# Non-local attention block: turned diagonal tiles split into two halves, and four chunks of g made at once in the head

## The chip, the cores and the metric

One core of one Trainium2 chip. The metric is the time of one execution in microseconds (us), median of several. TensorE multiplies matrices, VectorE and ScalarE work element by element, GpSimd too, and SyncE issues the DMAs.

## The reference

For each of 4 images x of 256 channels and n = 64 x 64 = 4096 places, after a group norm over 32 groups:

```python
g_x  = einsum('oc,bchw->bohw', g_w, x) + g_b          # 128 channels
f    = einsum('bnc,bcm->bnm', theta, phi)             # theta = x transposed, phi = x: f is symmetric
attn = softmax(f, axis=-1)
y    = einsum('bnm,bmc->bnc', attn, g_x)
wy   = einsum('oc,bchw->bohw', W_w, y) + W_b
wy   = batch_norm(wy) * gamma + beta                  # over images and places
out  = x + (wy + group_norm(x))
```

All arrays are fp32. The work lies in f (4096 x 4096 per image) and in attn times g.

## The kernel before

**Blocks and tiles.** The 4096 places are cut into NB = 8 chunks of W = 512. Block j computes y for the 512 places of chunk j. It takes TPB = 32 steps, one for each tile of 128 x 512 of the softmax's numerator; a step is numbered p = 32 j + i. Since f is symmetric, only the chunks (j, c) with c >= j are multiplied (`multiply`, L1135 to L1137). A product goes in three parts, high x high, high x low and low x high, each in the type fp32r; the halves of x are xh and xl. VectorE takes each product out of PSUM into a ring of 9 slots in SBUF (`take_f`, L930) and keeps a running maximum (L938); chunks with c > j are also spilled to DRAM.

**Two kinds of tiles.** `tile(p)` gives block, chunk, row and whether the tile is "left".
- A right tile is exponentiated on ScalarE in the ring (L760), turned by four transposes on TensorE into a PSUM bank (`turn`, L1177) and then split: ScalarE casts it to its high half phi (`split_hi`, L786), VectorE subtracts that from the bank to get the low half plo (`split_lo`, L965), and TensorE makes three products, gh x phi, gl x phi, gh x plo (L1205 to L1207). gh and gl are the halves of g.
- A left tile is already the way round that is needed. It is loaded from the spill (into lbuf or the free parts fy_c and fy_d), GpSimd subtracts the row maxima (L695), ScalarE exponentiates (`exp_left`, L775), and TensorE takes it in one fp32 product with the unsplit g, gf (L1201), which leaves two records in the trace. VectorE adds the left tiles up for the softmax's denominator (`add_left`, L978 for the first two, L982 for the others).
- The diagonal chunk (j, j) is symmetric in itself, so in blocks 1 to 6 its four tiles need no turning either. `turned_self` marks them: they are left tiles that stay in the ring. They are the turned diagonal tiles of the title, used in the first third of a block.

**What sets the order.** Every engine runs its own list of steps written out by the planners at the file's head; the engines meet only in semaphores. In step p TensorE turns the tile of step p + LAG (LAG = 2), makes the products planned for this step, and then calls `attend` for tile p. ScalarE at step s exponentiates left tile s + 3 and casts tile s + 2. VectorE at step p makes the low half of tile p first, then adds left tiles for step p + 1, takes products, and near a block's begin makes the reciprocal of the last block's sums (`invert`, L995, L998, L1000), which TensorE spreads in L1263. phi has 3 buffers, plo 2, products 2 banks. In the second half of the first three images the next image's statistics (L873), high and low halves (L736, L668) and first products come in between.

**The head.** Before the first step there are the statistics and halves of image 0 and the 32 products of its block 0. g is made in half chunks (`make_g`, L1157 to L1160) into the one bank sps, which VectorE empties into gf (`add_g`, L911) before the next one is made. `NEXT_G` is the chunks 0 and 1, made before the steps; chunks 2 to 7 are made at the steps that G_AT names, chunks 2 and 3 at steps 2, 3, 6 and 7, two steps' work ahead of their use. ScalarE casts a chunk to gh (`make_gh`, L750), GpSimd makes gl (L674).

## Time and profile before

| | |
|---|---|
| median of 3 runs | 2197.24 us (2196.96 to 2199.29) |
| profiled execution | 2195.28 us, span from first to last instruction 2193.5 us |
| granted TensorE clock, mean | 0.991 of full speed |
| TensorE busy | 2059.5 us, 94% |
| VectorE busy | 1556.7 us, 71% |
| ScalarE busy | 1090.8 us, 50% |
| GpSimd busy | 810.7 us, 37% |

The span is what the trace covers; the profiled execution's own time is 1.8 us longer. The engines work side by side, so their times don't add up. Matmul records overlap, since a record lasts until its result is out, while the next one has begun: what a matmul costs is read from start to start.

### The profile page before, as it was taken

The page shows a single profiled execution, that of the slowest core. Times are in us where ns is not written, and L with a number is a line of the kernel's source. Part 1 is how long each engine was busy: PE and PEld are TensorE (multiplying, and loading weights), DVE is VectorE, ACT ScalarE, POOL GpSimd, SP SyncE. Part 2 cuts the span into 40 slices and gives each one's busy share as a digit, 9 for nine tenths or more (in the row PEclk, how much of TensorE's full clock was granted, in tenths as well). Part 3 has the DMA queues.
Part 4 walks back from the last instruction along what each step waited for, and adds up shares of the span by engine and source line. Part 5 has one row for each costly group of instructions (what it writes and reads, how often), then busy time and mean ns, then how long its engine had stood idle before and what let it go on. Part 6 is the DMA issues. An engine that isn't in the chain of part 4 may idle for free.

```text
span 2193.5 us, 32307 instructions
## 1 busy us (share of the span) xinstructions
PE 2059.5 (94%) x9348; PEld 1454.6 (66%) x9348; DVE 1556.7 (71%) x3123; ACT 1090.8 (50%) x2234; POOL 810.7 (37%) x623
## 2 busy tenths in 40 slices
PE   5899999989999999999999999998999999999988
PEld 4686777755577777765667677765558777766433
DVE  5576777777766777786767677777776677777656
ACT  3344455555444445447444445545544444555644
POOL 3001223459602023448631122445850102345840
PEclk9999999999999999999999999999999999999999
DMA  3112234545512323554522223464541233346969
GB/s 139 77 77 81 103 121 130 173 150 178 178 45 87 115 98 110 165 175 138 197 72 93 87 92 112 129 200 137 191 150 49 87 120 102 110 130 218 344 236 356
DMA packets 108408, 304.50 MB, mean 139 GB/s; under 512 B 11584, under 2 KB 11968, under 8 KB 93888
## 3 DMA queue, kind: packets, MB, share of 16 engines
q1 hardware_dynamic: 108224, 302.30, 40.6%
q8 instruction: 84, 1.38, 0.2%
q14 instruction: 100, 0.82, 0.1%
HBM read 159.65 MB, written 142.61 MB: 138 GB/s over the span
## 4 chain that ended last, share of the span: by engine, by line
PE 68%; issue 11%; POOL 8%; ACT 5%; DVE 4%; DMA 3%; DVEq 0%; SPq 0%; POOLq 0%; ACTq 0%
PE bank L1201 12%; PE bank L1135 10%; PE bank L1137 9%; PE bank L1136 9%; PE bank L1177 7%; PE bank L1205 4%; PE bank L1207 4%; PE bank L1206 4%; POOL fy_d L695 3%; POOL fy_c L695 3%; ACT ring L760 2%; PE bank L1350 2%; PE bank L1271 2%; DVE plo L965 2%; DMA fy_c<-spill 2%
## 5 line engine op out<-in xcount | busy, mean ns | idle before, releaser
L786 ACT CAST phi<-bank 128x512 fp32r<-128x512 f32 x480 | 281.9, 588 | 765.7 <-PE bank L1177 764.7
L930 DVE TENSOR_SCALAR_CACHE_REDUCE ring<-bank 128x512 f32<-128x512 f32 x576 | 395.7, 688 | 209.3 <-PE bank L1137 164.0
L1135 PE MATMUL bank<-xh 128*128 128x512 f32 (+3 forms) x1152 | 512.8, 445 | 8.4 <-POOL xl L668 6.4
L1137 PE MATMUL bank<-xh,xl 128*128 128x512 f32 (+3 forms) x1152 | 436.1, 379 | 0.0
L965 DVE TENSOR_TENSOR plo<-bank,phi 128x512 fp32r<-128x512 f32 x480 | 327.2, 685 | 153.5 <-ACT phi L786 121.2
L1136 PE MATMUL bank<-xl,xh 128*128 128x512 f32 (+3 forms) x1152 | 433.1, 376 | 0.0
L1177 PEld LDWEIGHTS bank<-ident,ring 128*128 128x128 f32 x1920 | 231.6, 142 | 183.4 <-issue 109.2
L760 ACT ACTIVATE ring<-ring,nmax 128x512 f32<-128x512 f32 x480 | 345.8, 722 | 0.0
L1177 PE MATMUL bank<-ident,ring 128*128 128x128 f32 x1920 | 295.1, 277 | 43.7 <-DVE plo L965 22.5
L695 POOL TENSOR_TENSOR fy_d<-fy_d,maxrow 128x512 f32<-128x512 f32 x188 | 242.3, 1291 | 222.3 <-DMA fy_d<-spill 222.3
L695 POOL TENSOR_TENSOR fy_c<-fy_c,maxrow 128x512 f32<-128x512 f32 x200 | 259.0, 1297 | 167.0 <-DMA fy_c<-spill 166.6
L1135 PEld LDWEIGHTS bank<-xh 128*128 128x128 f32 x1152 | 218.1, 189 | 76.9 <-issue 29.3
L938 DVE TENSOR_TENSOR colmax<-bank,colmax 128x512 f32<-128x512 f32 x392 | 269.0, 686 | 0.0
L695 POOL TENSOR_TENSOR ring<-ring,maxrow 128x512 f32<-128x512 f32 x96 | 125.5, 1318 | 356.7 <-ACT maxrow L769 356.7
L1136 PEld LDWEIGHTS bank<-xl,xh 128*128 128x128 f32 x1152 | 219.0, 190 | 55.0 <-issue 29.2
L1137 PEld LDWEIGHTS bank<-xh,xl 128*128 128x128 f32 x1152 | 217.0, 188 | 42.1
L1205 PE MATMUL bank<-phi,gh 128*128 128x512 f32 x480 | 214.0, 446 | 19.2 <-DVE plo L965 18.8
L1201 PE MATMUL bank<-fy_c,gf 128*128 128x512 f32 x400 | 206.5, 599 | 4.2 <-DVE bank L982 3.0
L1201 PE MATMUL bank<-fy_d,gf 128*128 128x512 f32 x376 | 194.4, 599 | 4.7 <-DVE bank L982 3.7
L1207 PE MATMUL bank<-plo,gh 128*128 128x512 f32 x480 | 189.4, 394 | 0.0
L1206 PE MATMUL bank<-phi,gl 128*128 128x512 f32 x480 | 188.2, 392 | 0.0
L674 POOL TENSOR_TENSOR gl<-gf,gh 128x512 fp32r<-128x512 f32 x32 | 41.0, 1282 | 364.7 <-ACT gh L750 364.7
(115 smaller groups left out, 2716.9 us busy)
## 6 DMA issues: line engine op xcount, KB each, us to landing
spill<-ring SPq DMA_DIRECT2D x112, 1024.0 KB, 4.4
fy_c<-spill SPq DMA_DIRECT2D x200, 256.0 KB, 4.1
fy_d<-spill SPq DMA_DIRECT2D x188, 256.0 KB, 4.1
ring<-x_dram SPq DMA_DIRECT2D x40, 512.0 KB, 4.9
lbuf<-spill SPq DMA_DIRECT2D x60, 256.0 KB, 4.0
yd<-yn SPq DMA_DIRECT2D x32, 256.0 KB, 3.4
fx_a<-x_dram SPq DMA_DIRECT2D x16, 512.0 KB, 8.3
out_dram<-fx_a SPq DMA_DIRECT2D x16, 512.0 KB, 4.6
```

What stands on the lines that cost most here:

```text
L695: nc.gpsimd.tensor_tensor(left_at(w), left_at(w), maxrow[:, :], ALU.subtract).then_inc(left_sub, 1)
L760: nc.scalar.activation(ring[:, SLOT[u], t, :], ring[:, SLOT[u], t, :], ACT.Exp, bias=nmax[:, j % 3, t:t + 1], accum_out=rsum[:, j % 2, t, ...
L786: nc.scalar.copy(phi[:, HI_BUF[n], :], whole(p)).then_inc(hi_made, 1)
L930: last = nc.vector.tensor_scalar(ring[:, SLOT[u], t, :], src, 1.0, None, ALU.mult, ALU.max, accum_out=rowm[:, t, c:c + 1])
L965: nc.vector.tensor_tensor(plo[:, n % LOS, :], whole(p), phi[:, HI_BUF[n], :].bitcast(F32), ALU.subtract).then_inc(lo_made, 1)
L1135: nc.tensor.matmul(dst, xh[:, k, rows], xh[:, k, cols], start=(k == 0), stop=False)
L1136: nc.tensor.matmul(dst, xh[:, k, rows], xl[:, k, cols], start=False, stop=False)
L1137: last = nc.tensor.matmul(dst, xl[:, k, rows], xh[:, k, cols], start=False, stop=(k == K - 1))
L1177: last = nc.tensor.transpose(pps[:, n % 2, t * P:(t + 1) * P], ring[:, k, t, r * P:(r + 1) * P], ident[:, :])
L1201: nc.tensor.matmul(y, gf[:, c, r, :], left_at(LEFT_NO[p]), start=begin, stop=end).then_inc(tile_used, 1)
L1205: nc.tensor.matmul(y, gh[:, c, r, :], hi, start=begin, stop=False)
L1207: nc.tensor.matmul(y, gh[:, c, r, :], lo, start=False, stop=end).then_inc(tile_used, 1)
```

## The change

The turned diagonal tiles move from the list of tiles that are taken whole to SPLIT, the list of tiles that are cast, subtracted and taken in three products. They stay left tiles otherwise: GpSimd's subtraction, the exponential and the addition remain, and they are not turned by TensorE. Their source for the cast and the subtraction is the ring in SBUF (`whole`). SPLIT grows from 120 to 144 tiles per image. In the head the chunks 0 to 3 of g (FIRST_G) are made before the steps, the two half chunks of each in two banks, sps and lacc, and the casts to gh of chunks 0 and 1 stand behind six exponentials on ScalarE. lo_made counts in twos, with all its waits doubled.

```diff
-FULL = range(1, NB)
-SPLIT = [p for p in range(TILES) if not (tile(p)[3] and p // TPB in FULL)]
+SPLIT = [p for p in range(TILES) if not tile(p)[3] or turned_self(*tile(p)[:2])]
...
+FIRST_G = range(LAST_HEAD_G[0])
...
-            for c in NEXT_G:
-                make_gh(0, c, first=True)
             for s in range(FIRST_EXP, 0):
                 for x3 in EXPS_AT[s]:
                     exp_right(0, *x3)
+                if s + LAG == 0:
+                    for c in NEXT_G:
+                        make_gh(0, c, first=True)
...
+                made = lacc if first and h == 1 and c in FIRST_G else sps
+                nc.vector.tensor_reduce(gf[:, c, 2 * h:2 * h + 2, :], made.rearrange("p (t o c) -> p t c o", t=T // 2, o=2),
...
-                                        ALU.subtract).then_inc(lo_made, 1)
+                                        ALU.subtract).then_inc(lo_made, 2)
...
-                if p - 1 in G_AT:
+                if p - 1 in G_AT and not (first and G_AT[p - 1][0] in FIRST_G):
...
-            for c in NEXT_G:
+            for c in FIRST_G:
                 for h in range(2):
-                    add_g(0, c, h)
+                    add_g(0, c, h, first=True)
...
-                elif c + h > 0:
-
-                    pe.wait_ge(g_added, 2 * c + h)
+                elif c > 0:
+
+                    pe.wait_ge(g_added, 2 * c + h - (1 if c in FIRST_G else 0))
...
-                    pe.wait_ge(lo_made, b * NSPLIT + SPLIT_NO[p] + 1)
+                    pe.wait_ge(lo_made, b * (2 * NSPLIT) + 2 * SPLIT_NO[p] + 2)
...
-                if p in G_AT:
+                if p in G_AT and not (first and G_AT[p][0] in FIRST_G):
```

Where the instructions move: VectorE at the begin of block 5 (steps 161 to 163 of the loop over images), before. REGISTER_ALU rows compute the value of a wait; the line numbers of the changed file are 1 to 3 higher.

```order
L970 REGISTER_ALU
L978 TENSOR_TENSOR bank<-lbuf,ring 128x512
L992 REGISTER_ALU
L995 TENSOR_REDUCE lside<-bank 128x4
L998 TENSOR_TENSOR lsum<-lside,lsum 128x4
L1000 RECIPROCAL linv<-lsum 128x4
L928 REGISTER_ALU
L930 TENSOR_SCALAR ring,rowm<-bank 128x512
L938 TENSOR_TENSOR colmax<-bank,colmax 128x512
```

The same place on VectorE after the change:

```order
L967 TENSOR_TENSOR plo<-ring,phi 128x512
L972 REGISTER_ALU
L980 TENSOR_TENSOR bank<-lbuf,ring 128x512
L994 REGISTER_ALU
L997 TENSOR_REDUCE lside<-bank 128x4
L1000 TENSOR_TENSOR lsum<-lside,lsum 128x4
L1002 RECIPROCAL linv<-lsum 128x4
L930 REGISTER_ALU
L932 TENSOR_SCALAR ring,rowm<-bank 128x512
L940 TENSOR_TENSOR colmax<-bank,colmax 128x512
```

A subtraction with the inputs ring and phi now stands ahead of the first addition and of the reciprocal. Two more follow in steps 163 and 165, one in step 168.

ScalarE in the head, before (x6 is six instructions in a row):

```order
L736 CAST xh<-ring 128x2x512
L750 CAST gh<-gf 128x512 x2
L760 ACTIVATE ring,rsum<-ring,nmax 128x512 x6
L786 CAST phi<-bank 128x512
L760 ACTIVATE ring,rsum<-ring,nmax 128x512
```

And after:

```order
L736 CAST xh<-ring 128x2x512
L760 ACTIVATE ring,rsum<-ring,nmax 128x512 x6
L750 CAST gh<-gf 128x512 x2
L786 CAST phi<-bank 128x512
L760 ACTIVATE ring,rsum<-ring,nmax 128x512
```

The two casts of g moved behind the six exponentials.

## Rows read from the trace of the kernel before

**Rows 1.** The page: busy time, and the chain that ended last by engine

```profile
PE 2059.5 (94%) x9348; PEld 1454.6 (66%) x9348; DVE 1556.7 (71%) x3123; ACT 1090.8 (50%) x2234; POOL 810.7 (37%) x623
...
PE 68%; issue 11%; POOL 8%; ACT 5%; DVE 4%; DMA 3%; DVEq 0%; SPq 0%; POOLq 0%; ACTq 0%
```

**Rows 2.** Busy time by stretch: length, engines (instructions), clock, DMA share, GB/s

```profile
core 0: us, PE busy (x) PEld busy (x) DVE busy (x) ACT busy (x) POOL busy (x), PEclk, DMA share, GB/s
774.00:800.00 26.00, 25.83 (x128) 19.89 (x127) 19.68 (x42) 10.18 (x23) 7.47 (x6) 1.00 0.21 72
840.00:856.00 16.00, 16.00 (x80) 11.16 (x79) 11.85 (x24) 9.49 (x21) 9.96 (x9) 1.00 0.26 85
897.00:914.00 17.00, 17.00 (x83) 12.07 (x81) 13.40 (x26) 8.28 (x17) 12.30 (x11) 1.00 0.26 85
951.00:972.00 21.00, 18.00 (x75) 11.66 (x75) 19.70 (x40) 6.68 (x13) 14.36 (x13) 1.00 0.48 140
1013.00:1030.00 17.00, 14.86 (x55) 9.40 (x56) 13.77 (x25) 10.86 (x18) 17.00 (x13) 1.00 0.38 120
1984.00:1998.00 14.00, 13.96 (x69) 10.02 (x68) 10.58 (x24) 6.59 (x13) 13.96 (x11) 1.00 0.55 169
2031.00:2044.00 13.00, 11.54 (x43) 6.20 (x42) 8.93 (x15) 8.87 (x18) 10.82 (x9) 1.00 0.79 221
```

**Rows 3.** Groups by line and form: busy us, mean ns, idle before

```profile
L695 POOL TENSOR_TENSOR fy_c<-fy_c,maxrow 128x512 f32<-128x512 f32 x200 | 259.0, 1297 | 167.0 <-DMA fy_c<-spill 166.6
...
L1201 PE MATMUL bank<-ring,gf 128*128 128x512 f32 x192 | 98.2, 596 | 4.5 <-DVE bank L982 4.1
...
L978 DVE TENSOR_TENSOR bank<-lbuf,ring 128x512 f32<-128x512 f32 x20 | 27.8, 1390 | 0.4 <-ACT lbuf L775 0.3
...
L978 DVE TENSOR_TENSOR bank<-fy_c,lbuf 128x512 f32<-128x512 f32 x4 | 2.8, 704 | 0.0
L978 DVE TENSOR_TENSOR bank<-ring 128x512 f32<-128x512 f32 x4 | 2.8, 696 | 0.0
```

**Rows 4.** Timeline of TensorE: start, us from start to end

```profile
299.63 0.40 PE L1205 MATMUL bank<-phi,gh 128*128 128x512 f32 x1
...
300.32 0.60 PE L1177 MATMUL bank<-ident,ring 128*128 128x128 f32 x4
...
331.31 1.02 PE L1201 MATMUL bank<-lbuf,gf 128*128 128x512 f32 x2
332.17 1.02 PE L1201 MATMUL bank<-ring,gf 128*128 128x512 f32 x2
```

**Rows 5.** Timeline of all engines, block 5 of the second image

```profile
956.72 1.26 DVE L978 TENSOR_TENSOR bank<-lbuf,ring 128x512 f32<-128x512 f32 x1
...
957.39 1.71 POOL L695 TENSOR_TENSOR fy_d<-fy_d,maxrow 128x512 f32<-128x512 f32 x1
...
959.38 0.65 PE L1263 MATMUL bank<-ident,linv 128*128 128x128 f32 x4 [1.37 <-DVE linv L1000]
...
966.60 1.12 PE L1201 MATMUL bank<-ring,gf 128*128 128x512 f32 x2 [1.28 <-DVE bank L982]
```

**Rows 6.** Timeline of all engines, the head

```profile
76.67 0.39 PE L1157 MATMUL bank<-wgs,xh 128*128 128x256 f32 x1 [1.49 <-DVE gf L911]
...
82.56 0.62 ACT L750 CAST gh<-gf 128x512 fp32r<-128x512 f32 x1 [3.32 <-DVE gf L911]
...
86.06 1.97 PE L1177 MATMUL bank<-ident,ring 128*128 128x128 f32 x8 [4.26 <-ACT ring L760]
...
87.33 0.56 ACT L786 CAST phi<-bank 128x512 fp32r<-128x512 f32 x1
...
89.50 0.78 PE L1205 MATMUL bank<-phi,gh 128*128 128x512 f32 x1
...
97.86 0.28 PE L1157 MATMUL bank<-wgs,xh 128*128 128x256 f32 x1
...
98.79 0.60 PE L1177 MATMUL bank<-ident,ring 128*128 128x128 f32 x4
```

**Rows 7.** Busy time and granted clock (the number after POOL)

```profile
87.00:100.00 13.00, 12.28 (x65) 10.54 (x63) 5.18 (x10) 6.54 (x17) 0.00 (x0) 0.75 0.00 1
```

More of the change, by code:

```diff
@@ L906, in group, with add_g @@
                                             1.0, None, ALU.add).then_inc(gnp_made, 1)
-            def add_g(n, c, h):
+            def add_g(n, c, h, first=False):
                 dve.wait_ge(g_made, n * (2 * NB) + 2 * c + h + 1)
-                nc.vector.tensor_reduce(gf[:, c, 2 * h:2 * h + 2, :], sps.rearrange("p (t o c) -> p t c o", t=T // 2, o=2),
+                made = lacc if first and h == 1 and c in FIRST_G else sps
+                nc.vector.tensor_reduce(gf[:, c, 2 * h:2 * h + 2, :], made.rearrange("p (t o c) -> p t c o", t=T // 2, o=2),
                                         AX.X, ALU.add).then_inc(g_added, 1)
@@ L1149, in make_g @@
                     shared_free(b, "g", c, h)
-                elif c + h > 0:
-                    pe.wait_ge(g_added, 2 * c + h)
+                elif c > 0:
+                    pe.wait_ge(g_added, 2 * c + h - (1 if c in FIRST_G else 0))
+                made = lacc if first and h == 1 and c in FIRST_G else sps
                 for r in range(2 * h, 2 * h + 2):
                     rows = slice(c * W + r * P, c * W + (r + 1) * P)
-                    both = sps[:, r % 2 * 2 * CI:(r % 2 + 1) * 2 * CI]
-                    high = sps[:, r % 2 * 2 * CI:r % 2 * 2 * CI + CI]
+                    both = made[:, r % 2 * 2 * CI:(r % 2 + 1) * 2 * CI]
+                    high = made[:, r % 2 * 2 * CI:r % 2 * 2 * CI + CI]
                     nc.tensor.matmul(both, xh[:, 0, rows], wgs[:, 0, :], start=True, stop=False)
@@ L1171, in turn @@
                 if n >= 2:
-                    pe.wait_ge(lo_made, b * NSPLIT + SPLIT_NO[IN_PSUM[n - 2]] + 1)
+                    pe.wait_ge(lo_made, b * (2 * NSPLIT) + 2 * SPLIT_NO[IN_PSUM[n - 2]] + 2)
                 elif not first:
-                    pe.wait_ge(lo_made, b * NSPLIT + SPLIT_NO[IN_PSUM[n - 2]] + 1 - NSPLIT)
+                    pe.wait_ge(lo_made, b * (2 * NSPLIT) + 2 * SPLIT_NO[IN_PSUM[n - 2]] + 2 - 2 * NSPLIT)
                 k = SLOT[CHUNK_NO[j, c]]
@@ L1313, in _ @@
             pe.wait_ge(wg_lo, 1)
-            for c in NEXT_G:
+            for c in FIRST_G:
                 for h in range(2):
```

## The prediction

> **What bounds the kernel now.** I read the page first. TensorE is busy 94% of the span, VectorE 71%, and 68% of the chain that ended last is on TensorE [rows 1]. So work taken from TensorE should pay. But the chain also holds 8% GpSimd, 5% ScalarE and 4% VectorE: there are places where TensorE follows another engine. An average over the span hides the places of the change, so I went on to the view of busy time by stretches and asked for those in which the turned diagonal tiles are used, in blocks 2 to 6 of the second image and 5 and 6 of the last [rows 2]. There the picture differs by block: in block 2 VectorE has 19.68 of 26.00 us, in block 4 13.40 of 17.00, in block 5 19.70 of 21.00. In block 5 VectorE, not TensorE, is the full engine (TensorE 18.00 of 21.00). The reader is to see that the same edit meets a full TensorE in blocks 2 to 4 and a full VectorE or GpSimd in blocks 5 and 6.
>
> **The tiles on TensorE.** 96 tiles change (4 in each of 6 blocks and 4 images; the fp32 product leaves two records each, hence x192 in [rows 3]). In the timeline an fp32 product takes 0.86 us from its start to the next one's (331.31 to 332.17), and the three products of a split tile 0.69 us (299.63 to 300.32) [rows 4]. So TensorE gets 0.17 us per tile back, 16.3 us in all if it were the bound at each; that is the most the tiles can give. The mean of a record (596 ns) would have said 1.19 us for the fp32 product, since records overlap; starts are what counts.
>
> **The tiles on ScalarE and VectorE.** Each tile gets a cast to the high half on ScalarE, which stands at 50% in the page and is ahead in these stretches; I cost it at nothing. Its cover is the two steps by which the split runs ahead of the product; were that gone, the cast would cost its own length. Each tile also gets a subtraction on VectorE, 128x512, both inputs in SBUF. No such subtraction runs before, but an addition of this size and kind does, L978 [rows 3]: 696 ns with ring and ring, 704 with fy_c and lbuf, 1390 on average with lbuf and ring. The difference is GpSimd: the one at 956.72 took 1.26 us while GpSimd was inside a subtraction, and GpSimd's next one, at 957.39, took 1.71 us [rows 5] where 1.30 is the mean [rows 3]. The two engines exclude each other here. The mean over the 28 L978 instructions is (20 x 1.390 + 4 x 0.696 + 4 x 0.704) / 28 = 1.19 us. Bounds: 0.70 us when GpSimd is idle, 1.39 us where it is not. I take 1.19 us, since the new instructions stand in the very same stretches; 4 of them are 4.8 us per stretch (2.8 to 5.6).
>
> The Trainium skill, "SBUF — State Buffer on-chip working memory", section "Who interferes with whom", says the same and speaks against this change: a VectorE instruction with two SBUF inputs and a GpSimd one that reads SBUF lock each other out for a whole instruction. It says besides that an instruction with one SBUF input doesn't take part, so the existing split tiles, whose source is in PSUM, are no measure for the new ones: by their 0.69 us a stretch would get 2.8 us, by the rule up to 5.6. The trace agrees with the lock.
>
> Now stretch by stretch: VectorE's sum with 4.8 us more, against the stretch's length [rows 2]. Where it still fits, the stretch gets 4 x 0.17 = 0.7 us shorter; where it doesn't, it gets longer by the excess.
> - Block 2: 19.68 + 4.8 = 24.5 of 26.0. It fits with little room, so I count -0.3. Block 1 has no row here; it starts like block 2, with the fewest left tiles of all, and I let it fit: -0.7.
> - Block 3: 11.85 + 4.8 = 16.7 of 16.0: 0.7 too much, against 0.7 saved: 0.
> - Block 4: 13.40 + 4.8 = 18.2 of 17.0: +1.2; I take +1.
> - Block 5 (images 0 to 2): 19.70 + 4.8 = 24.5 of 21.0: +3.5. Here I also followed the order. The first new subtraction stands right ahead of L978 and the reciprocal chain [rows 5]. Both need the port, so after the first has waited for GpSimd, L978 waits for GpSimd's next instruction as well: the reciprocal (L1000) comes some 1.8 us later, and with it L1263 at 959.38, for which TensorE already sat idle 1.37 us. Two more subtractions stand before the addition that releases L1201 at 966.60, for which TensorE already waits 1.28 us. Together 1.8 + 2 x 1.1 = 4.0. I take +4.0.
> - Block 6 (images 0 to 2): 13.77 + 4.8 = 18.6 of 17.0, GpSimd busy 17.00 of 17.00: +1.8.
> - Block 5 of the last image, without the next image's statistics: 10.58 + 4.8 = 15.4 of 14.0: +1.5. Block 6: 8.93 + 4.8 = 13.7 of 13.0: +1.
>
> An image 0 to 2 thus gets -0.7 - 0.3 + 0 + 1 + 4.0 + 1.8 = +5.8 us, the last +2.5, together +19.9 us. What queues behind the subtraction on VectorE is the addition of the next left tile, the taking of the products out of PSUM and, at a block's begin, the reciprocal; TensorE waits for each.
>
> **The head.** Before, TensorE makes 4 half chunks of g, each waiting for VectorE to empty the only bank (the second starts at 76.67). ScalarE casts chunk 1 at 82.56, and only behind it come six exponentials, of which the first turning needs four; it starts at 86.06, the first cast of a tile at 87.33, the first product with a tile at 89.50 [rows 6]. From the end of the cast of chunk 1 (83.1) to 87.33 the six take 4.2 us. After the change they come first, from about 76.2 (VectorE releases the second half chunk at 76.67, right behind the row maxima), and end near 80.5. TensorE makes 8 half chunks in two banks. A half chunk is 0.93 us of TensorE (97.86 to 98.79) [rows 6]. The third starts at 76.67, where the second does now; from there one is made under VectorE's addition, so that two take some 1.95 us instead of one: the eighth ends near 82.5. From the first turning to the first product it takes 3.44 us now (86.06 to 89.50), at a low clock and with exponentials in between; I estimate 2.5 us at the full clock, so the first product comes at about 85.0, 4.5 us earlier. Four half chunks are gone from steps 2, 3, 6 and 7, where TensorE is full: 4 x 0.93 = 3.7 us. And the clock: from 87 to 100 us it is 0.75 on average [rows 7], so it is at 1.2 GHz for half of these 13 us, up to about 93.5; TensorE had sat idle 4.26 us before 86.06. The work from 89.5 to 93.5 would take 2.0 us, half, less at 2.4 GHz. Since TensorE now pauses for about 1 us only, I expect that it stays at 2.4 GHz. Head: -4.5 - 3.7 - 2.0 = -10.2 us (-8.2 if the clock falls again; -3.7 if ScalarE's new order brings nothing).
>
> The Trainium skill, "TensorE: Matmul & The Clock Gate", section "What's actually happening", puts the low clock down to idleness before it; by that rule the 2.0 us come back with the shorter pause, and the row agrees, with the low clock standing behind the 4.26 us.
>
> **The sum.** 19.9 - 10.2 = +9.7 us on the profiled execution's 2195.28 us (its span is 2193.5): 2205.0 us. The same sums with a subtraction at its lower bound (2.8 us per stretch) fit everywhere but in block 5: about -2 us an image and -4 in the last, tiles -10.2, in all 2175; at its upper bound (5.6) the tiles come to about +35, in all 2220. The median of the runs shown is 1.96 us above that execution, so I expect a median of 2207 us, 0.45% slower. A measurement of this kernel can tell about 0.2% (4.4 us) from no change.
>
> **The rivals.** (a) Faster: VectorE's extra work is absorbed. VectorE is idle 29% of the span and TensorE, not it, ends most waits; it may catch up in the steps behind each stretch. Then the tiles give between 0 and -16.3 us and the head -10.2: 2169 to 2185, most likely 2181 with the tiles at -4. For it: VectorE is idle 6.3 us of 26.0 even in block 2's stretch [rows 2]. Against: in block 5 TensorE already waits for VectorE [rows 5]. It decides if the tiles cost less than 5.7 us in all, that is if the stretches of blocks 5 and 6 grow by less than 1 us each instead of the 5.8 above for both.
> (b) The halves cancel: at 1.0 us for a subtraction (4.0 us per stretch) the tiles come to +2.8 us an image and +1 in the last, +9.4, against the head's -10.2: 2196, no change.
> (c) The lock hits in full: every subtraction waits for a whole GpSimd instruction and GpSimd, which is full in block 6, falls behind as well. At +4 us in blocks 4 and 6 and +6 in block 5: 4 x 13 = 52, less 6 in blocks 1 to 3, less the head's 10: 2197 + 36 = 2233.
> (d) The clock falls again inside the kernel: TensorE's new waits in block 5 (1.37 + 1.8 = 3.2 us before L1263) come near the 4.26 us after which the clock fell in the head. If it falls there, the work of the next 6.5 us or so runs at half speed, 3 us more in each of 3 images: 2216. The page "TensorE: Matmul & The Clock Gate" of the Trainium skill says that an idle stretch throttles.
>
> **How the numbers follow.** My forecast (+4.4 to +22 us) 0.50, (d) 0.07, (c) 0.08, (b) within 0.2% 0.14, (a) 0.21. Slower 0.65, same 0.14, faster 0.21. The range leaves out the deeper half of (a) and the upper half of (c): 2184 to 2226.
>
> **What would show it.** In the profile after: the three products at 0.69 us from start to start; the new subtraction on average at 1.0 to 1.3 us, longest in block 6, and GpSimd's at 1.7 where they meet; TensorE's first product with tiles near 85 us, with the clock near full from 75 to 100; the stretch of block 5 some 25 us instead of 21, the blocks 1 to 3 unchanged within 1 us each. Wrong would be: subtractions at 0.7 us throughout, a block 5 of the old length, or a head that comes no earlier because ScalarE stands in the casts of g in its new place.

## The result, and the profile after

| | before | after |
|---|---|---|
| median | 2197.39 us (4 runs, 2196.96 to 2199.29) | 2239.54 us (4 runs, 2236.23 to 2241.52) |
| ratio | | 1.0189, 95% interval 1.0171 to 1.0206 |
| span of the profiled execution | 2193.5 us | 2238.4 us |
| mean granted clock | 0.991 | 0.986 |

The change makes the kernel 1.9% slower. The direction was forecast; 2239.54 us lies above the range (2184 to 2226).

The page of the changed kernel, busy time by engine and the chain that ended last, against [rows 1]:

```profile
PE 2061.5 (92%) x9444; PEld 1480.9 (66%) x9444; DVE 1646.0 (74%) x3219; ACT 1143.9 (51%) x2330; POOL 826.5 (37%) x623
...
PE 64%; issue 13%; POOL 7%; DVE 7%; ACT 5%; DMA 3%; DVEq 0%; SPq 0%; ACTq 0%; POOLq 0%
```

VectorE has 89.3 us more work and is busy 74% instead of 71%: nothing here looks full. Of the 44.9 us that the span grows, TensorE's idle time (span less busy) takes 42.9: 134.0 us before, 176.9 after. VectorE's share of the last chain goes from 4% to 7% and TensorE's falls from 68% to 64%. The groups by line and form (busy us, mean ns, idle before with its releasers), against [rows 3]:

```profile
L967 DVE TENSOR_TENSOR plo<-bank,phi 128x512 fp32r<-128x512 f32 x480 | 327.0, 685 | 152.8 <-ACT phi L786 76.4 <-PE bank L1210 39.9 <-PE bank L1204 22.0
...
L695 POOL TENSOR_TENSOR fy_c<-fy_c,maxrow 128x512 f32<-128x512 f32 x200 | 267.0, 1337 | 166.3 <-DMA fy_c<-spill 166.0
...
L967 DVE TENSOR_TENSOR plo<-ring,phi 128x512 fp32r<-128x512 f32 x96 | 96.9, 1009 | 6.4 <-ACT phi L786 6.2
...
L980 DVE TENSOR_TENSOR bank<-lbuf,ring 128x512 f32<-128x512 f32 x20 | 29.7, 1484 | 0.0
```

The new subtraction (plo from ring) takes 1009 ns on average, the old one from PSUM 685. GpSimd's subtraction goes from 1297 to 1337 ns, the addition L980 from 1390 to 1484. The view of waits shows who waits for the low halves (us in all, number, longest):

```profile
PEld bank L1208 <- DVE plo L967: 105.0, 106, 2.8
...
PE bank L1208 <- DVE plo L967: 54.4, 61, 2.3
```

Before, the same lines of the same view (L1205 for L965) gave 46.5 us in 61 waits and 18.8 us in 26. So TensorE's waits for a low half grew by 36 us in the products and by 59 in the weight loads (which wait for it too, and start earlier); the same time is in both, so they don't add up.

**Where along the kernel.** TensorE spreads the last block's reciprocals (L1263 before, L1266 after) one step after each block's begin. The starts of these 32 rows are marks: the one of block 5 in the second image stands at 959.38 us before [rows 5]; that of block 6 in the same image is shown below (L1266 at 1035.83). The change of the time from one mark to the next, after against before, worked out from those rows, in us:

```
interval from block   1      2      3      4      5      6      7    0 (next image)
image 0            +0.53  -0.70  +2.86  +2.90  +7.18  +2.49  +0.17  +0.68
image 1            +0.21  -0.66  +2.79  +2.60  +6.44  +2.47  +1.67  +1.50
image 2            +0.20  -0.68  +3.08  +2.85  +5.43  +2.54  -2.62  +0.93
image 3            +0.14  -0.60  +3.27  +2.24  +6.00  +1.31  -0.02
sum                 +1.1   -2.6  +12.0  +10.6  +25.0   +8.8   -0.8   +3.1
```

The first mark, behind the head, comes 10.74 us earlier, and the sums add 57.2. Only block 2 gets what the three products save (4 x 0.17 = 0.68 us). Blocks 3 to 6 lose, block 5 most, and the last image as much as the others. Single entries hold up to 3 us that have nothing to do with the change: the -2.62 of block 7 in the third image stands in the head alone too (-2.78), since the kernel before, and not the changed one, has a stretch at a granted clock of 0.50 there.

### The profile page after: what moved, and what is told of

Its sections match the earlier page's. It is cut to its first block, busy times and chain, and to the rows that moved or that the text cites. A ratio compares the mean times of both kernels' runs of the same rounds, so it can differ in the third digit from the quotient of the medians.

```text
span 2238.4 us, 33110 instructions
## 1 busy us (share of the span) xinstructions
PE 2061.5 (92%) x9444; PEld 1480.9 (66%) x9444; DVE 1646.0 (74%) x3219; ACT 1143.9 (51%) x2330; POOL 826.5 (37%) x623
## 4 chain that ended last, share of the span: by engine, by line
PE 64%; issue 13%; POOL 7%; DVE 7%; ACT 5%; DMA 3%; DVEq 0%; SPq 0%; ACTq 0%; POOLq 0%
PE bank L1137 9%; PE bank L1139 9%; PE bank L1204 9%; PE bank L1138 9%; PE bank L1180 7%; PE bank L1208 4%; PE bank L1210 4%; PE bank L1209 4%; POOL fy_d L695 3%; DVE plo L967 3%; POOL fy_c L695 2%; ACT ring L760 2%; PE bank L1353 2%; PE bank L1274 2%; ACT phi L786 1%
## 5 line engine op out<-in xcount | busy, mean ns | idle before, releaser
L695 POOL TENSOR_TENSOR fy_d<-fy_d,maxrow 128x512 f32<-128x512 f32 x188 | 247.8, 1320 | 235.7 <-DMA fy_d<-spill 235.7
L695 POOL TENSOR_TENSOR fy_c<-fy_c,maxrow 128x512 f32<-128x512 f32 x200 | 267.0, 1337 | 166.3 <-DMA fy_c<-spill 166.0
L1208 PE MATMUL bank<-phi,gh 128*128 128x512 f32 x576 | 263.9, 458 | 54.7 <-DVE plo L967 54.4
L1210 PE MATMUL bank<-plo,gh 128*128 128x512 f32 x576 | 228.6, 397 | 0.0
L1209 PE MATMUL bank<-phi,gl 128*128 128x512 f32 x576 | 227.0, 394 | 0.0
L1208 PEld LDWEIGHTS bank<-phi,gh 128*128 128x128 f32 x576 | 109.3, 190 | 118.2 <-DVE plo L967 105.0
```

Source lines behind the costliest of these rows:

```text
L695: nc.gpsimd.tensor_tensor(left_at(w), left_at(w), maxrow[:, :], ALU.subtract).then_inc(left_sub, 1)
L1208: nc.tensor.matmul(y, gh[:, c, r, :], hi, start=begin, stop=False)
L1209: nc.tensor.matmul(y, gl[:, c, r, :], hi, start=False, stop=False)
L1210: nc.tensor.matmul(y, gh[:, c, r, :], lo, start=False, stop=end).then_inc(tile_used, 1)
```

## The experiments

Each ratio is to the kernel before, run beside it on the same chip (medians there 2198.67, 2196.48, 2196.74 and 2198.64 us).

**The two parts apart.** `e1_head_only` sets SPLIT back:

```diff
-SPLIT = [p for p in range(TILES) if not tile(p)[3] or turned_self(*tile(p)[:2])]
+SPLIT = [p for p in range(TILES) if not tile(p)[3]]
```

> The head's part alone: four chunks of g at once and the casts behind the exponentials, the turned diagonal tiles as before in one fp32 product. Every theory expects 10.7 us less than before, 2186.7 us, as the marks of the changed kernel stood 10.7 us earlier at the end of block 0. Only if the head hides what the tiles do would it be otherwise.

Measured: 2187.6 us, ratio 0.9945 (0.9925 to 0.9965). `e2_tiles_only` undoes the head (NEXT_G made in the one bank and cast ahead of the exponentials, as before) and keeps the tiles.

> The tiles' part alone, the head as before. If the two parts add up: 2239.5 + 10.7 = 2250 us. If the earlier start only moves waits that come later anyway, less: 2240 us.

Measured: 2248.5 us, 1.0227 (1.0193 to 1.026). So the head gives 11 us and the tiles cost 50 to 52 us, and the parts add up. The page of `e1_head_only` (TensorE idle 2186.4 - 2057.0 = 129.4 us):

```profile
PE 2057.0 (94%) x9348; PEld 1454.3 (67%) x9348; DVE 1556.5 (71%) x3123; ACT 1091.4 (50%) x2234; POOL 811.5 (37%) x623
```

**The subtraction left out.** In `e3_no_vector` the third product takes the high half again (the low part of these tiles is left out) and VectorE has no new work:

```diff
-                if p in SPLIT_NO:
+                if p in PSUM_NO:
                     split_lo(b, p, first)
...
-                hi, lo = phi[:, HI_BUF[n], :], plo[:, n % LOS, :]
+                hi = phi[:, HI_BUF[n], :]
+                lo = plo[:, PSUM_NO[p] % LOS, :] if p in PSUM_NO else hi
```

> The changed kernel without VectorE's subtraction for the 96 turned diagonal tiles (their third product takes the high half again, so the low half is left out of the result; TensorE waits for ScalarE's cast instead). Queue theory (VectorE's added time, and what stands behind it, is the whole loss): the three products then give their 0.15 to 0.17 us each, 2197.4 - 10.7 - 15 = 2172 us. ScalarE theory (the casts hold its exponentials and wait for phi's buffers): most of the loss stays, above 2210 us.

Measured: 2181.96 us, 0.9923 (0.9898 to 0.9949), that is 5.6 us under the head alone. ScalarE's casts are not the cause; VectorE's subtractions cost 2239.5 - 2182.0 = 58 us. Its page:

```profile
PE 2045.4 (94%) x9444; PEld 1472.3 (68%) x9444; DVE 1556.1 (71%) x3123; ACT 1142.9 (52%) x2330; POOL 811.4 (37%) x623
```

TensorE has the same instructions here as in the change, so the two pages divide the 58 us (profiled spans 2180.2 and 2238.4 us): it is idle 134.8 against 176.9 us, that is 42 us of waiting, and busy 2045.4 against 2061.5 us, 16 us in which the same work takes longer. The granted clock is 0.991 here and 0.986 there, which makes 20 and 31 us not granted, so the clock accounts for at most 12 of the 16; products behind a wait also have longer records (0.50 us against 0.40).

And of the 16.3 us that TensorE saves only some 6 reach the end even with nothing in the way, by the medians; the queue theory's 2172 was too low.

**The lock.** In `e4_psum_source` the subtraction reads a PSUM bank in place of the ring (the low part is then of other data):

```diff
-                nc.vector.tensor_tensor(plo[:, n % LOS, :], whole(p), phi[:, HI_BUF[n], :].bitcast(F32),
+                src = whole(p) if p in PSUM_NO else yps[:, (p // TPB + 1) % 2, :]
+                nc.vector.tensor_tensor(plo[:, n % LOS, :], src, phi[:, HI_BUF[n], :].bitcast(F32),
```

> The changed kernel, but VectorE's new subtraction takes its first input from a PSUM bank (the y of the block before, so the low halves of the turned diagonal tiles are wrong) in place of the ring; same place, same waits, one input in SBUF. Lock theory (the exclusion with GpSimd makes the loss): the instruction takes 0.69 us, GpSimd is not slowed, and most of the loss goes, 2205 us or less. Queue theory: VectorE gets 96 x 0.32 = 31 us of its 97 us back, about a third to a half of the 55 us loss: 2215 to 2225 us.

Measured: 2209.28 us, 1.0048 (1.0028 to 1.0068), between the two theories. Its groups:

```profile
L968 DVE TENSOR_TENSOR plo<-bank,phi 128x512 fp32r<-128x512 f32 x576 | 392.0, 685 | 162.4 <-ACT phi L786 90.8 <-PE bank L1211 33.5 <-PE bank L1205 24.2
...
L695 POOL TENSOR_TENSOR fy_c<-fy_c,maxrow 128x512 f32<-128x512 f32 x200 | 257.3, 1289 | 166.1 <-DMA fy_c<-spill 166.1
```

The 576 subtractions now take 685 ns on average and GpSimd is back below 1.30 us. So 30 of the 58 us go with what VectorE and GpSimd cost each other when both inputs lie in SBUF, and 27 are left for subtractions of 0.69 us. By the marks block 5 still loses 4.7 to 5.2 us in each image, block 3 1.3 in three of the four and block 6 1.5 to 1.9.

**Not waited for.** In `e5_no_wait` all subtractions are made, but for these tiles TensorE waits for the cast only and its third product takes the high half:

```diff
-                if p in SPLIT_NO:
+                if p in PSUM_NO:
                     pe.wait_ge(lo_made, b * (2 * NSPLIT) + 2 * SPLIT_NO[p] + 2)
+                elif p in SPLIT_NO:
+                    pe.wait_ge(hi_made, b * NSPLIT + SPLIT_NO[p] + 1)
```

ScalarE and VectorE wait for lo_made here before they reuse a buffer, since TensorE no longer stands for it.

> The change as it is, but TensorE's third product of a turned diagonal tile takes the high half again, and TensorE waits for the cast and not for the subtraction; VectorE still makes all 96 subtractions, in the same place (their results are read by nobody, so the low parts of these 24 tiles an image are left out). Without them at all the kernel took 2181.96 us. Direct wait (TensorE loses its time waiting for the low halves themselves): below 2200 us, with blocks 3 to 6 within 2 us each of the kernel without subtractions. Displaced work (what costs is that the subtraction pushes back what stands behind it in VectorE's order: taking products, the chain of the reciprocal, the subtractions of the other tiles): 2225 us or more, because all of that still happens.

Measured: 2231.16 us, 1.0157 (1.0135 to 1.0179). Only 8 of the 58 us go with TensorE's own wait for these low halves (block 5: +15.6 instead of +25.0). In the view of waits TensorE's products wait for low halves 23.1 us instead of 54.4, but it waits 25.5 us for linv instead of 14.7 and 18.8 us for VectorE's additions instead of 7.8: what stands behind the subtraction is late instead.

**One step earlier.** `e6_early`:

```diff
-                if p in SPLIT_NO:
+                if p in SPLIT_NO and p not in LEFT_NO:
                     split_lo(b, p, first)
+                if p + 1 in SPLIT_NO and p + 1 in LEFT_NO:
+                    split_lo(b, p + 1, first)
```

> The change as it is, but VectorE subtracts a turned diagonal tile one step earlier, right behind the subtraction of the tile before and ahead of the products that it takes in that step. The same instructions, in another order. Place (TensorE waits because the subtraction stands behind other work of VectorE that itself waits for TensorE): 2205 to 2225 us against 2239. Displaced work or lock (the 1.0 us and the port lost count wherever they stand): within 5 us of 2239; slower than 2245 if the products that it takes are now the late ones.

Measured: 2247.87 us, 1.0226 (1.0208 to 1.0244), slower than the change itself. TensorE waits 29.9 us for low halves instead of 54.4, but behind VectorE's taking of products (L1144 in the change) 31.2 us instead of 17.1: what had stood ahead of the subtraction is late instead.

**One block alone.** `e7_block5_only` and `e8_block2_only` add `and p // TPB == 5` (or 2) to the condition on turned_self in SPLIT.

> The new head, and halves for the turned diagonal tiles of block 5 alone (16 of 96); those of the other blocks keep one fp32 product. The marks of the whole change gave block 5 +25.0 us over the four images. Cost made in the block itself: 2187.6 + 25 = 2213 us (2208 to 2218). Cost built up by the blocks ahead, VectorE coming to block 5 late: 2204 us or less. My rule on record (block 5 +4.0 in three images, +1.5 in the last): 2201 us.

Measured: 2215.13 us, 1.0071 (1.005 to 1.0091): 27.5 us over the head alone. The cost is made in the block itself. By the marks 18.1 us lie in the interval of block 5 and 6.8 in that of block 4, since the tile of step 1 comes just ahead of the mark; in the table above, too, the intervals of blocks 3 to 5 hold the first tile of the next block.

> The new head, and halves for the turned diagonal tiles of block 2 alone. The marks of the whole change gave block 2 -2.6 us over the four images, the head alone took 2187.6 us. If block 2 wins what TensorE saves whatever the others do: 2185 us (2183 to 2187). If the gain of block 2 only made up for a late block 1: 2187.6 us or more.

Measured: 2189.66 us, 0.9962 (0.9945 to 0.9979). The marks show block 2 at -2.4 us as expected, but 2.7 us more in the last image's block 5, and 2.9 in block 7 of the first, eat it up; by the medians nothing is gained on the head alone.

**VectorE's other work cut, behind the subtraction.** `e9_small_adds`, with `e10_small_adds_fp32` as its control (the same edit on the head alone):

```diff
-                    nc.vector.tensor_tensor(lacc, left_at(w), lacc, ALU.add).then_inc(left_added, 1)
+                    p = LEFT[w]
+                    m = 4 if p // TPB in (3, 4, 5, 6) and p % TPB <= 10 and tile(p)[1] != p // TPB else W
+                    nc.vector.tensor_tensor(lacc[:, :m], left_at(w)[:, :m], lacc[:, :m], ALU.add).then_inc(left_added, 1)
```

> The whole change, but in the first 11 steps of blocks 3 to 6 VectorE adds 4 of 512 columns of each left tile that is not a diagonal one and not among the block's first two (14 tiles an image; the rest of their column sums is left out). That takes 56 x 0.62 = 35 us off VectorE, in the steps in which the subtractions stand, and changes nothing for TensorE, ScalarE and GpSimd. Full stretch (TensorE waits because VectorE has no gap at the start of these blocks, and each microsecond put in there comes out in full): blocks 3 to 6 lose 56 us in the whole change and get back 0.6 to 1.0 of the 35, so 2239 - 21 to 35 = 2204 to 2218 us. Wait for the low half itself or the lock as such: within 8 us of 2239.

> The control: the new head and one fp32 product for each turned diagonal tile, with the same 56 additions of 4 columns (the rest of these column sums is left out). Against 2187.6 us with whole additions. Full stretch already before the change: 2172 to 2182 us, since TensorE already waited at the start of these blocks and part of that goes. VectorE had room there before the change and was only pushed over by it: within 3 us of 2187.6.

Measured: 2240.11 us, 1.0194 (1.017 to 1.0218), and the control 2185.47 us, 0.9942 (0.9925 to 0.996). The page of the first:

```profile
PE 2067.3 (92%) x9444; PEld 1484.5 (66%) x9444; DVE 1622.5 (72%) x3219; ACT 1143.5 (51%) x2330; POOL 824.6 (37%) x623
```

VectorE had 23.5 us less to do in just these steps, and the time is the same. The theory of a full VectorE, which asked for 21 to 35 us back, falls. But not quite nothing came back: TensorE's idle time is 171.4 us (2238.7 - 2067.3) instead of 176.9. What it saved there it lost in slower work, 2067.3 us busy instead of 2061.5, at a granted clock of 0.983 instead of 0.986.

**VectorE's other work cut, ahead of the subtraction.** `e13_small_colmax`, with its control `e14_small_colmax_fp32`; `narrow` is set for p in the first 11 steps of blocks 3 to 6:

```diff
-                    last = nc.vector.tensor_tensor(cm, src, before, ALU.max)
+                    m = 4 if narrow else W
+                    last = nc.vector.tensor_tensor(cm[:, :m], src[:, :m], before[:, :m], ALU.max)
```

> The whole change, but in the first 11 steps of blocks 3 to 6 VectorE takes the column maximum of 4 of 512 columns of each product (47 instructions in all, about 28 us; the rest of these maxima is left out). They stand behind VectorE's wait for a product and ahead of the next step's subtraction; the additions that were cut before stood behind it. Chain within a step (a subtraction costs where it is the last link of TensorE to VectorE to TensorE): 2210 to 2228 us, and less than half of that on the control. Work of VectorE is of no account wherever it stands, only the lock counts: within 4 us of 2239.5.

> The control: the new head, one fp32 product for each turned diagonal tile, the same 47 column maxima of 4 columns (the rest left out). Both theories: 2187.6 us less 0 to 8.

Measured: 2227.72 us, 1.0127 (1.0102 to 1.0153), and the control 2187.15 us, 0.9942 (0.9919 to 0.9964). The page of the first:

```profile
PE 2056.2 (92%) x9444; PEld 1478.8 (66%) x9444; DVE 1623.4 (73%) x3219; ACT 1143.8 (51%) x2330; POOL 826.0 (37%) x623
```

22.6 us less for VectorE, nearly the same as in the run above, but the kernel is 11.8 us faster than the whole change, and the control is as long as the head alone. That is the slow end of what the chain was expected to give. By the marks block 5 goes from +25.0 to +14.9 and block 6 from +8.8 to +5.1; blocks 3 and 4, where maxima were cut too, gain nothing (+12.6, +11.2).

That looks as if the place of the work decided and not its amount, but the pages don't bear it out in this size. TensorE is idle 171.4 us with the additions cut and 168.8 with the maxima cut, only 2.6 us apart; 11.1 of the 13.7 us between the two profiled executions are TensorE's busy time, at granted clocks of 0.983 and 0.988. Block 5 of the first image, between its marks, with the head alone, in the change, and with the maxima cut (the clock is the number after POOL):

```profile
430.36:490.03 59.67, 52.31 (x223) 33.33 (x223) 45.47 (x96) 32.88 (x61) 33.49 (x24) 1.00 0.47 140
435.73:502.65 66.92, 54.94 (x226) 36.53 (x226) 49.36 (x100) 36.10 (x66) 34.26 (x24) 0.95 0.37 115
435.71:498.93 63.22, 51.74 (x227) 34.08 (x227) 47.25 (x100) 36.10 (x66) 34.38 (x24) 1.00 0.41 121
```

TensorE is idle there 7.36, 11.98 and 11.48 us. Of the 3.7 us that the cut gives back in this interval, 0.5 is waiting and 3.2 is TensorE's own work at the full clock. In block 6 it is waiting: 2.82, 1.42 and 2.83 us idle in the first three images in the change, 0.61, 0.67 and 0.49 with the maxima cut (1.68, 1.66 and 1.70 with the additions cut).

Three timelines of one place show how a link ahead of the subtraction differs from one behind it: block 6 of the second image, from TensorE's projection (L1274 to L1276) to the first product of the fourth turned diagonal tile there. In the changed kernel:

```profile
1045.95 1.02 PE L1274 MATMUL bank<-yn,wwt 128*128 128x512 f32 x2
...
1047.13 0.70 DVE L1011 BATCH_NORM_STATS2 bns<-bank 128x512 f32 x1 [0.61 <-PE bank L1274]
...
1047.74 0.67 DVE L932 TENSOR_SCALAR_CACHE_REDUCE ring<-bank 128x512 f32<-128x512 f32 x1
...
1048.34 0.69 DVE L940 TENSOR_TENSOR colmax<-bank,ring 128x512 f32<-128x512 f32 x1
...
1048.94 1.44 DVE L967 TENSOR_TENSOR plo<-ring,phi 128x512 fp32r<-128x512 f32 x1
...
1050.43 0.50 PE L1208 MATMUL bank<-phi,gh 128*128 128x512 f32 x1 [1.21 <-DVE plo L967]
```

With the additions cut (`e9_small_adds`):

```profile
1042.61 0.15 DVE L986 TENSOR_TENSOR bank<-fy_d,bank 128x4 f32<-128x4 f32 x1
...
1043.54 1.02 PE L1276 MATMUL bank<-yn,wwt 128*128 128x512 f32 x2
...
1044.71 0.70 DVE L1013 BATCH_NORM_STATS2 bns<-bank 128x512 f32 x1 [1.15 <-PE bank L1276]
...
1046.53 1.42 DVE L967 TENSOR_TENSOR plo<-ring,phi 128x512 fp32r<-128x512 f32 x1
...
1048.01 0.50 PE L1210 MATMUL bank<-phi,gh 128*128 128x512 f32 x1 [1.20 <-DVE plo L967]
```

With the column maxima cut (`e13_small_colmax`):

```profile
1038.28 1.02 PE L1275 MATMUL bank<-yn,wwt 128*128 128x512 f32 x2
...
1039.44 0.70 DVE L1012 BATCH_NORM_STATS2 bns<-bank 128x512 f32 x1 [0.62 <-PE bank L1275]
...
1040.66 0.16 DVE L941 TENSOR_TENSOR colmax<-bank,ring 128x4 f32<-128x4 f32 x1
...
1040.73 0.72 DVE L968 TENSOR_TENSOR plo<-ring,phi 128x512 fp32r<-128x512 f32 x1
...
1041.51 0.50 PE L1209 MATMUL bank<-phi,gh 128*128 128x512 f32 x1
```

VectorE works in order and stands at L1011 until TensorE's projection is done. From then on everything is a chain: statistics, product taken, column maximum, subtraction, and TensorE waits at its end. In the second timeline the short addition only makes VectorE reach L1013 earlier and wait there 1.15 us instead of 0.61; from projection to product it takes 4.47 us instead of 4.48. In the third it takes 3.23 us with no wait of TensorE. The short instruction is a link of this chain and gives 0.53 of the 1.25 us; the other 0.72 come from the lock, since the subtraction now begins just ahead of GpSimd's next instruction (1.74 us) and takes 0.72 us instead of 1.44.

**Other places in the block.** `e11_later_halves` moves the turned diagonal tiles of blocks 3 to 5 to steps 4 to 10, `e12_later_fp32` does so for the head alone:

```diff
-        left += [((0.13 if j == 1 else 0.07) + 0.035 * q, j, q) for q in range(T)]
+        left += [({1: 0.13, 2: 0.07, 6: 0.07}.get(j, 0.16) + 0.035 * q, j, q) for q in range(T)]
```

> The whole change, with the turned diagonal tiles of blocks 3, 4 and 5 at steps 4, 6 or 7, 8 and 10 in place of 1 or 2 to 8: behind the stretch in which VectorE has no gap. Against its control with one fp32 product: in the old places these three blocks lost 48 us of the 52 that the tiles cost. Full stretch: the difference to the control is 15 to 38 us. A price for each subtraction wherever it stands: 48 to 56 us.

> The control of the later places: the new head, one fp32 product for each turned diagonal tile, those of blocks 3, 4 and 5 at steps 4, 6 or 7, 8 and 10. All theories: 2187.6 us within 8, since the same instructions run in another order; a faster one would be the version to take.

Measured: 2225.34 us, 1.0134 (1.0111 to 1.0157), and the control 2202.92 us, 1.0029 (1.0016 to 1.0042). The halves cost 22 us there instead of 52. But the control is 15 us slower than the head alone, outside what I expected, so it is no version to take; why it is slower was not looked into.

**Early in three blocks only.** `e15_early_345` is `e6_early` with `j in (3, 4, 5)` added to both conditions.

> The whole change, with the subtraction of a turned diagonal tile one step earlier in blocks 3, 4 and 5 alone. By the marks of the kernel that had it in all blocks, these three blocks lose 30.4 us there against 47.6 in the change, the others more. The costs of blocks add up: 2239.5 - 17 = 2222 us (2217 to 2228). The gain in blocks 3 to 5 came from the blocks ahead being late: 2235 us or more.

Measured: 2239.12 us, 1.0181 (1.0159 to 1.0203): no gain, a miss. The marks say how I misread them: with early subtractions the interval of block 2 goes to +7.2 us though its order is untouched, because block 3's first subtraction now stands at its step 1, ahead of the reciprocal that the mark waits for. The loss had moved to the other side of a mark.

**Half the length.** In `e16_half_width` the subtraction of these tiles covers 256 columns (the other half of the low part is left out):

```diff
-                nc.vector.tensor_tensor(plo[:, n % LOS, :], whole(p), phi[:, HI_BUF[n], :].bitcast(F32),
+                m = W // 2 if p in LEFT_NO else W
+                nc.vector.tensor_tensor(plo[:, n % LOS, :m], whole(p)[:, :m], phi[:, HI_BUF[n], :m].bitcast(F32),
```

> The whole change, but the subtraction of a turned diagonal tile covers 256 of 512 columns (the other half of its low part is left out), in the same place, with the same waits, 0.35 to 0.5 us in place of 1.0. Price by length (each tenth of a microsecond on the chain comes out): about half of the 52 us, 2208 to 2220 us. Price by event (waiting behind a GpSimd instruction, a semaphore round): above 2228 us.

Measured: 2231.05 us, 1.0139 (1.0114 to 1.0163). Its group:

```profile
L968 DVE TENSOR_TENSOR plo<-ring,phi 128x256 fp32r<-128x256 f32 x96 | 70.9, 739 | 6.4 <-ACT phi L786 6.2
```

Half the columns took 739 ns on average, not 0.35 to 0.5 us, and gave 8.5 us back (TensorE idle 166.6 us instead of 176.9, but busy 2066.4 instead of 2061.5). That is the side of the price by event. The median is 420 ns here and 689 in the change, and in both runs 41 of the 96 subtractions are the long ones: the average stands 0.32 us above the median in both. So the half length takes off the instruction's own time, 0.27 us, and nothing of what meeting GpSimd adds.

## Why the prediction was wrong

**The head was right.** Predicted -10.2 us, measured -10.74 by the first mark, and 11 us by the medians of the head alone. The timeline of the head after, against [rows 6]:

```profile
77.04 0.72 ACT L760 ACTIVATE ring<-ring,nmax 128x512 f32<-128x512 f32 x1 [36.51 <-DVE nmax L959]
...
83.54 1.04 PE L1180 MATMUL bank<-ident,ring 128*128 128x128 f32 x8
...
86.08 0.47 PE L1208 MATMUL bank<-phi,gh 128*128 128x512 f32 x1
```

and the clock, against [rows 7] (it is the number after POOL):

```profile
87.00:100.00 13.00, 13.00 (x80) 11.29 (x79) 8.14 (x19) 7.56 (x18) 1.29 (x1) 1.00 0.01 2
```

The first product comes at 86.08, 3.4 us earlier and not 4.5, but a microsecond of that was lost ahead of the change: TensorE's first product for g starts at 75.08 us in this execution and at 74.10 before. From there to the first product with a tile it takes 11.0 us instead of 15.4, that is 4.4 us less, and so in every run with the new head; the head alone has:

```profile
74.06 0.28 PE L1160 MATMUL bank<-wgs,xh 128*128 128x256 f32 x1
...
85.06 0.47 PE L1208 MATMUL bank<-phi,gh 128*128 128x512 f32 x1
```

So the 85.0 of the prediction was right. From turning to product it takes 2.54 us (predicted 2.5), and the clock stays at 2.4 GHz, as forecast. In the head alone the second product comes 6.2 us earlier and the tenth 10.8, so the clock gave 1.8 us (predicted 2.0) and the four half chunks, with what else changed in those steps, 4.6 (predicted 3.7).

**What three products save: priced right, realised in part.** In the timeline they take 0.70 us from start to start:

```profile
1041.58 0.40 PE L1208 MATMUL bank<-phi,gh 128*128 128x512 f32 x1
...
1042.28 0.59 PE L1204 MATMUL bank<-fy_c,gf 128*128 128x512 f32 x1
```

Without the subtraction 5.6 us of 16.3 reach the end. By the marks, `e3_no_vector` against the head alone, most intervals of blocks 1 to 5 are 0.5 to 0.9 us shorter, as priced, some 11 us in all; the head and the other intervals are 5 us longer there.

**The subtraction's own price was not too low.** I took 1.19 us; it is 1.009 us on average, near the 1.0 of rival (b), for which I had the tiles at +9.4 us. They cost 52. (55 of the 96 take their 0.69 us, 41 are longer, up to 2.70.)

**The step that failed** is the rule of the sum, "VectorE's sum with 4.8 us more, against the stretch's length", with "where it still fits, the stretch gets 4 x 0.17 = 0.7 us shorter". Block 3 was set at 0 and block 4 at +1 us per image; their intervals grew by 2.8 to 3.3 and 2.2 to 2.9. The last image's block 5 was set at +1.5, with VectorE at 10.58 of 14.00 us [rows 2], and grew by 6.0, as much as in the images where VectorE had 19.70 of 21.00. VectorE's idle time is not free: it is mostly waiting, in order, for something that TensorE or ScalarE has just made, and what follows is a chain back to TensorE. The waits show it: between the marks TensorE's products wait for low halves 3.3 us in block 3, 5.1 in block 4 and 7.1 in block 6 (all four images together), where with the head alone they don't wait at all, and 31.1 us in block 5 instead of 13.4. And two cuts of VectorE's work, 23.5 and 22.6 us in just these steps, took only 5.5 and 8.1 us off TensorE's idle time. So the sum over a stretch bounds what VectorE must be given, not what a new link costs. The sum also put the clock inside the kernel at nothing (it was left to rival (d)), and that TensorE's own work took 16 us longer with the subtractions than without was in none of its terms.

**Where my order argument was used, it held but was too short.** In block 5 I added the chain of the reciprocal (+1.8) and two subtractions (+2.2). The whole is 5.4 to 7.2 us in the first three images. The chain of the reciprocal looks in the changed kernel, at the begin of block 6, as I had described it for block 5:

```profile
1031.25 1.48 DVE L967 TENSOR_TENSOR plo<-ring,phi 128x512 fp32r<-128x512 f32 x1 [0.67 <-ACT phi L786]
...
1032.12 1.74 POOL L695 TENSOR_TENSOR ring<-ring,maxrow 128x512 f32<-128x512 f32 x1
...
1032.65 1.77 DVE L980 TENSOR_TENSOR bank<-lbuf,ring 128x512 f32<-128x512 f32 x1
...
1033.83 1.71 POOL L695 TENSOR_TENSOR fy_c<-fy_c,maxrow 128x512 f32<-128x512 f32 x1
...
1035.83 0.65 PE L1266 MATMUL bank<-ident,linv 128*128 128x128 f32 x4 [2.08 <-DVE linv L1002]
```

This part was sized well, but only part of it shows as a wait for linv. At the begin of block 5 in the second image TensorE waits first for the low half of the first tile and then for linv, 2.96 us in all where it was 1.37:

```profile
966.65 0.50 PE L1208 MATMUL bank<-phi,gh 128*128 128x512 f32 x1 [0.88 <-DVE plo L967]
...
969.69 1.11 PE L1266 MATMUL bank<-ident,linv 128*128 128x128 f32 x4 [2.08 <-DVE linv L1002]
```

Where TensorE does not wait for the low half (`e5_no_wait`), the whole stands in one wait, 1.9 us longer than before:

```profile
971.41 0.65 PE L1271 MATMUL bank<-ident,linv 128*128 128x128 f32 x4 [3.27 <-DVE linv L1004]
```

What was short is the two subtractions at 1.1 us, and the clock: in block 5 TensorE's idle time grew by 3.1 to 4.6 us in these images (from 7.4 us), and the rest of the 5.4 to 7.2 is its own work at granted clocks of 0.93 to 0.96.

**The rivals.** (c), the lock in full, gave 2233 us and comes nearest in size, with a chance of 0.08. (Its own terms, 4 + 4 + 6 = 14 us an image and not 13, would have given 2237.) Half of it is true: without the lock 30 of the 58 us are gone. But it is not that every subtraction waits for a whole GpSimd instruction (55 of 96 don't wait at all): the lock costs VectorE 1009 - 685 = 324 ns each, 31 us, and GpSimd 826.5 - 810.7 = 16 us in all. The Trainium skill, "SBUF — State Buffer", section "Who interferes with whom", has the lock for two SBUF inputs and not for one; the trace agrees (1009 against 685 ns). What the lock costs the kernel hangs on who waits behind the two instructions. (d), the falling clock, with a chance of 0.07, did happen, in block 5 of all three images as it said, and in other places too, though behind waits of about 2 us, where it had counted on one of 3.2. The windows around the wait for L1266 above:

```profile
1033.80:1035.80 2.00, 0.00 (x0) 0.00 (x0) 1.93 (x5) 1.91 (x3) 2.00 (x3) 1.00 0.00 0
1035.80:1037.80 2.00, 1.98 (x9) 1.66 (x10) 1.82 (x4) 1.97 (x4) 2.00 (x2) 0.73 0.00 0
1037.80:1039.80 2.00, 2.00 (x6) 1.22 (x4) 1.55 (x1) 2.00 (x5) 2.00 (x2) 0.50 0.00 0
```

TensorE waits 2.08 us, and behind that the granted clock falls to 0.50, 1.2 GHz. Over the span the clock not granted is (1 - 0.986) x 2238 = 31 us after and (1 - 0.994) x 2186 = 13 us with the head alone. The pages divide the 52 us: TensorE is idle 47.5 us more (176.9 against 129.4) and busy 4.5 us more (2061.5 against 2057.0), although three products in place of one save it 16.3; so its work as such took some 21 us longer, up to 18 of them by the clock. (d) had 9 us for it. (a) and (b) are out: no block but the second absorbed the work.

**What stays open.** Why the 27 us without the lock lie so much in block 5 was not tested by itself; in `e4_psum_source` TensorE's products wait for low halves 31.3 us in block 5, as long as with the lock, while in blocks 3 and 4 that falls to 0.3 and 0.9 us. Why the clock falls behind one wait of 2 us and not behind another is open too (in `e5_no_wait` it falls behind the 3.27 us before L1271 in the first image and stays full behind the same 3.27 us in the second), and with it most of the difference between the two cuts. And that the halves cost less in other places (22 against 52 us) was shown with a control that is slower itself. The version to take is the head alone, 0.9945 of the time before; no kernel that computes everything beat it by more than the measurement tells.

## What to carry to other kernels

Before adding work to an engine with idle time, look at what ends that idle time and at what follows it: if it ends with the bottleneck's own result and the bottleneck waits at the other end, an instruction in between is paid for however idle the engine is on average (here 96 subtractions of 1.0 us on an engine 74% busy cost 58 us). Cost a new instruction as a link of that chain, one step at a time, and keep busy-time sums for a lower bound. When two runs are compared, divide the time into the bottleneck's idle and busy time first: here the profiled executions of the two cuts of VectorE's work were 13.7 us apart, and 11.1 of them were TensorE's busy time. And when one part of a change gains (here the head, 11 us) and another loses (the tiles, 50 to 52), run them apart before judging either.

## What the runs showed of the hardware

The lock costs both sides, and can cost more than an instruction's length. At the same place:

```profile
1037.98 2.36 POOL L668 TENSOR_TENSOR xl<-ring,xh 128x1024 fp32r<-128x1024 f32 x1
...
1038.24 2.65 DVE L967 TENSOR_TENSOR plo<-ring,phi 128x512 fp32r<-128x512 f32 x1 [0.63 <-ACT phi L786]
...
1040.30 1.75 POOL L695 TENSOR_TENSOR ring<-ring,maxrow 128x512 f32<-128x512 f32 x1
```

The subtraction begins 0.26 us after a GpSimd instruction twice its size, ends 0.55 us behind it, and the next GpSimd instruction takes 1.75 us instead of the 1.28 that it has elsewhere in these timelines. I had expected such a subtraction at 1.39 us at most. Shortening the instruction doesn't shorten what the lock adds: half the columns took 739 ns on average against 1009, with medians of 420 and 689 ns, so the lock added 0.32 us on average in both.
